# A fused attention, state-space and expert layer on one core: a chunk's preparation two slots forward, one expert layer per slot, and half of the key masks on ScalarE

## The chip, the cores and the metric

The kernel runs on one core of a Trainium2 chip. The metric is the device time of one execution in microseconds, as the median of several executions. Engines are named as in the profile: PE is TensorE, DVE is VectorE, ACT is ScalarE, POOL is GpSimd, SP is SyncE, which only issues DMAs here.

## The reference, cut to what matters

The input is four images of 64x64 tokens with 64 channels, all float32.

```python
h = window_attention(x)                    # 8x8 windows, 8 heads of 8 channels, 2D rotary, output projection
h = h + mamba(layernorm(h))                # RMS norm, in-projection to xc and z, causal conv over 4 taps, silu
#   delta = softplus(xc @ Wd + bd); dA = exp(delta * A); state h_t = dA_t*h_{t-1} + x_t*delta_t*B_t
#   y = (sum over 16 states of h_t*C_t + xc*D) * silu(z); out projection, residual
h = h + experts(layernorm(h))              # router of 6 experts, top 2; each expert has 3 layers with relu
```

## The kernel before, in words

The 16384 tokens are cut into 16 chunks of 1024 (CH). One call of `body(c, odd)` on each engine is one chunk's time of 32 slots (SLOTS), numbered n. Every engine has its own `body`, with its own order of helper calls inside a slot; the order of instructions on an engine is therefore written out by hand, and the engines meet through semaphores only. Six bodies run ahead of the hardware loop (c = -3 to 2), the loop does c = 3 to 12 two chunks at a time, and five more bodies close (c = 13 to 17).

A slot n of body c holds work of up to five chunks:

- **The scan of chunk c**, one unit (8 channels by 16 states, half a chunk of time) per slot. ACT writes the decay of unit n+2 to PSUM (`decay`, L767; it waits for the scan of unit n). DVE scans unit n (L1005) and multiplies B into a later unit (`feed`, L996). POOL multiplies with C (`weigh`, L1252). PE gathers four units at a time (`collect`, L449). SP loads `dl` for unit n+5 and `xd` for unit n+6, each broadcast to 128 partitions.
- **The attention of chunk c+3** (from slot 9; slots 0 to 8 finish chunk c+2, by `attention_at`), in its own slots s = n-9. PE turns the input (s=0), makes keys and queries (`keys_queries`, s=1 and 3, L466 and L470) and values (s=5, 6). DVE rotates them into `rot` (L1033, s=2 and 3) and POOL adds the two parts (L1265, s=4, which is slot 13). SP then copies the 16 head blocks of the keys into `k_heads` (`heads`, L341: 2 window halves by 8 heads, 6, 5 and 5 of them in slots 13, 14, 15) and the two halves of the queries into `q_diag` (`queries`, L350, slot 14). `k_heads` has, for every head, 64 key columns that are zero outside the head's 8 channels. The scores of window w (`scores`, L527, s = 9+2w, the first of them in slot 18) wait for all 18 of these DMAs. DVE takes the maximum (`maxima`, L1023, two slots on), ACT spreads it into `shift`, PE makes the transposed scores (`turned`, L537 and L538), ACT the exponentials (`probsT`, L775), PE the values (`values`, L551), ACT copies them out (`pv`).
- **The preparation of chunk c+1** (`prepare` on PE, ACT, DVE and POOL): transposes of the normed input (n0, n1 in slots 4, 5), the convolution (conv0, conv1 in slots 6, 7; L571 and L572 on PE, L844 on ACT), z (slots 8, 9), silu between two loads of activation tables (slot 9, L757 and L853), delta's projection (slots 11, 12; L863 and L864), exp and log of softplus (slot 13, L867), xdel's first step on DVE (slot 14, L1072) and eight steps on POOL (slots 14 to 21, L1301 to L1308). SP writes delta and xdel to DRAM (`keep`, slots 20 and 22). The second half of C is made in slot 2 of the chunk's own body (`second`: PE L594, ACT c_rep).
- **The normalisation of chunk c+2** (`normalize`), and **the experts of chunk c-1** (`experts`, `layers`, `route`): the output projection mo (PE L608, slot 4), the norm, the router (DVE `route`, slots 15 to 19: some twenty short operations, L1110 to L1166), then three pairs of experts with two layers each (h1_0, h2_0, ..., h2_2). A layer fills two PSUM banks, bank 7 (F) and bank 6 (G). LAYERS_PE says in which slot PE makes a layer and whether early or late in it; LAYERS_ACT says for each of the two banks when ACT empties it. Both halves of a table are served by the two calls of `layers` in the PE and ACT bodies.

Bank 6 also serves n0, n1, conv0, conv1, z0, d0, d1, c0 and c1, so each of these waits until ACT has emptied the one before; z1 is in bank 7, with the F uses.

```python
def attention_at(c, n):
    return (c + 3, n - 9) if n >= 9 else (c + 2, n + 23)
```

Of the kernel before, what the change touches and what calls it, by code (L numbers as in the profile page):

```python
# [21 lines left out]
NW = IMG // WIN  # L22
# [16 lines left out]
        ("keep", NCH + 1)]  # L39
ONCE = [("bv_rep", 128), ("wp_row", 64), ("normw", 1), ("conv_in", 128), ("conv_tap", 256), ("z_in", 128),  # L40
        ("d_skip", 1), ("a_log", NU), ("rb1", 1), ("rw2", E), ("headmask", 8)]
# [22 lines left out]
for _w in range(NW):  # L64
# [12 lines left out]
LAYERS_ACT = {(14, False): ("h1_0", 0), (14, True): ("h1_0", 1), (16, True): ("h2_0", 0), (17, False): ("h2_0", 1),  # L77
              (17, True): ("h1_1", 0), (18, False): ("h1_1", 1), (19, False): ("h2_1", 0), (19, True): ("h2_1", 1),
              (20, False): ("h1_2", 0), (20, True): ("h1_2", 1), (21, False): ("h2_2", 0), (21, True): ("h2_2", 1)}
# [38 lines left out]
def tower(nc, x, packed, select, out):  # L118
    with ExitStack() as ctx:
# [114 lines left out]
        heads_in = sig("heads_in", 18 * 16)  # L234
# [70 lines left out]
        def _(sp):  # L305
# [60 lines left out]
            def body(c, odd):  # L366
                for n in range(SLOTS):
# [15 lines left out]
                    if has(c + 1):  # L383
                        if n == 20:
                            keep(c + 1, 0)
                        if n == 22:
                            keep(c + 1, 1)
# [37 lines left out]
        def _(pe):  # L425
# [95 lines left out]
            def scores(k, w):  # L521
# [3 lines left out]
                if w == 0:  # L525
                    pe.wait_ge(heads_in.sem, heads_in.at(k, 288))
# [29 lines left out]
            def prepare(k, q, n):  # L556
                for s, i2 in ((4, 0), (5, 1)):
# [7 lines left out]
                for h in range(2):  # L565
                    at = BAND * h
                    if n == 6 + h:
# [6 lines left out]
                    if n == 8:  # L574
# [8 lines left out]
                    if n == 11 + h:  # L583
# [12 lines left out]
            def second(k, q, n):  # L596
                if n == 2:
# [68 lines left out]
            def layers(k, n, late, before):  # L666
                name = LAYERS_PE.get((n, late))
# [43 lines left out]
            def body(c, odd):  # L711
# [4 lines left out]
                for n in range(SLOTS):  # L716
# [22 lines left out]
                    if has(c - 1):  # L739
                        layers(c - 1, n, True, before_layers)  # L740
# [716 lines left out]
```

## Time and profile before

| | |
|---|---|
| median of 3 runs | 2001.69 us (1990.23 to 2002.55) |
| the profiled execution's own time | 2010.24 us |
| its span in the profile | 2008.4 us |
| instructions | 31457 |
| busy share of the span | PE 71%, DVE 66%, POOL 60%, ACT 52% |
| granted TensorE clock, mean | 0.779 of full speed |

The profile is of one execution. A row of a timeline gives start, duration, engine, line, operation, tiles, count, and in brackets how long the engine stood idle before it and what ended that. Each engine's rows stand in the order in which its body issues them, so a slot can be found by counting the scans (L1005) or POOL's L1252. The first scan of chunk 0 starts near 225 us; before it three bodies hold attention and preparation alone.

### The profile page before, as it was taken

The numbers are of one execution on the slowest core, as the hardware profiler recorded it, in microseconds if no ns is written. First come the engines' busy times: TensorE is split into PE (matmuls) and PEld (weight loads), VectorE is DVE, ScalarE is ACT, GpSimd is POOL, SyncE is SP. The second block draws the span as 40 slices with busy tenths as digits, with TensorE's granted clock in tenths as the row PEclk, the third lists the DMA queues.
The fourth block names the chain that finished last, engine by engine and source line by source line (L and its number), as shares of the span: only waits on it lengthen the run. The fifth ranks groups of instructions, "written<-read, shape, count | busy, mean of one in ns | idle before, by whom it ended". The sixth has DMA issues, their size and how long they took to land. (4 is left out here: it accounts for less than half of the span.)

```text
span 2008.4 us, 31457 instructions
## 1 busy us (share of the span) xinstructions
PE 1430.9 (71%) x8148; PEld 654.9 (33%) x8148; DVE 1327.5 (66%) x1835; ACT 1049.3 (52%) x1956; POOL 1207.1 (60%) x1665
## 2 busy tenths in 40 slices
PE   3655757796977777686868777686868778566566
PEld 1442424252433334242423334242433334121121
DVE  1111568777678776877677776878577776868851
ACT  1223556546565654656565654656465655554432
POOL 1003375756667674766677674766567675877651
PEclk9776968777788877787988877787887878675755
DMA  2000556554656564555646465555546565676720
GB/s 63 2 16 28 165 183 207 162 162 141 190 148 207 159 194 145 167 177 149 190 145 203 149 198 148 168 178 152 176 136 202 159 188 153 191 202 205 215 78 6
DMA packets 223979, 306.55 MB, mean 153 GB/s; under 512 B 88141, under 2 KB 88345, under 8 KB 223641
## 3 DMA queue, kind: packets, MB, share of 16 engines
q1 hardware_dynamic: 223768, 304.19, 50.5%
q8 instruction: 78, 1.28, 0.3%
q14 instruction: 133, 1.08, 0.2%
HBM read 274.75 MB, written 20.97 MB: 147 GB/s over the span
## 5 line engine op out<-in xcount | busy, mean ns | idle before, releaser
L1252 POOL TENSOR_TENSOR hc<-hs,c_rep 128x512 f32<-128x512 f32 x512 | 654.7, 1279 | 539.8 <-DVE hs L1005 539.8
L1005 DVE TENSOR_TENSOR_SCAN hs<-bank,state,xd 128x512 f32<-128x512 f32 x512 | 651.5, 1275 | 38.1 <-issue 15.6
L767 ACT ACTIVATE bank<-dl,a_neg 128x512 f32<-128x512 f32 x512 | 350.5, 687 | 186.2 <-DVE hs L1005 167.2
L996 DVE TENSOR_TENSOR xd<-xd,bank 128x512 f32<-128x512 f32 x512 | 336.9, 663 | 49.0 <-PE bank L439 43.2
L527 PE MATMUL bank<-k_heads,q_diag 128*128 128x512 f32 x256 | 182.8, 804 | 145.5 <-DMA k_heads<-rot 103.3
L1023 DVE TENSOR_REDUCE neg_max<-bank 128x8 f32<-128x512 f32 x128 | 88.2, 689 | 266.2 <-PE bank L527 255.0
L537 PE MATMUL bank<-q_diag,k_heads 128*128 128x128 f32 x1024 | 212.3, 333 | 20.7 <-ACT shift L760 20.7
L537 PEld LDWEIGHTS bank<-q_diag,k_heads 128*128 128x128 f32 x1024 | 182.8, 217 | 98.6 <-issue 63.7
L775 ACT ACTIVATE probsT<-bank 128x512 f32<-128x512 f32 x128 | 76.4, 597 | 240.5 <-PE bank L538 240.5
L449 PE MATMUL bank<-hc,wts 128*32 128x512 f32 x1024 | 169.3, 721 | 6.4 <-POOL hc L1252 6.2
L1324 POOL TENSOR_TENSOR ew<-ew,e 128x512 f32<-128x512 f32 x96 | 121.3, 1264 | 55.0 <-ACT e L760 55.0
L684 PE MATMUL bank<-fT,wts 64*128 64x512 f32 x192 | 81.7, 939 | 99.6 <-ACT ew L942 82.1
L538 PE MATMUL bank<-ident_b,shift 128*128 128x128 bf16 x512 | 121.2, 237 | 0.0
L527 PEld LDWEIGHTS bank<-k_heads,q_diag 128*128 128x128 f32 x256 | 47.2, 226 | 202.9 <-issue 95.4
L551 PE MATMUL bank<-v_diag,probsT 128*64 128x18 f32 x2048 | 85.6, 217 | 36.3 <-ACT probsT L775 32.0
L551 PEld LDWEIGHTS bank<-v_diag,probsT 128*64 128x64 f32 x2048 | 73.7, 142 | 99.9 <-issue 58.1
L760 ACT ACTIVATE shift<-neg_max 128x512 bf16<-128x512 f32 x128 | 79.5, 621 | 38.8 <-DVE neg_max L1023 38.8
L1033 DVE SCALAR_TENSOR_TENSOR rot<-bank,wts 128x512 f32<-128x512 f32 x64 | 45.1, 746 | 74.5 <-PE bank L470 74.2
L594 PE MATMUL bank<-xz,wts 128*128 128x512 f32 x128 | 85.7, 757 | 8.7 <-ACT xz L853 7.7
L571 PE MATMUL bank<-xnT,conv_w 128*128 128x512 f32 x64 | 54.4, 945 | 40.4 <-ACT xnT L760 27.1
L939 ACT ACTIVATE e<-bank,wts 128x512 f32<-128x512 f32 x96 | 62.7, 675 | 38.4 <-PE bank L684 38.1
L760 ACT ACTIVATE pv<-bank 128x72 f32<-128x72 f32 x128 | 29.4, 230 | 92.6 <-PE bank L551 90.9
(175 smaller groups left out, 2442.1 us busy)
## 6 DMA issues: line engine op xcount, KB each, us to landing
xd<-xdel_rows SPq DMA_DIRECT2D x512, 256.0 KB, 3.9
dl<-delta_rows SPq DMA_DIRECT2D x512, 256.0 KB, 3.6
delta_rows<-delta SPq DMA_DIRECT2D x16, 512.0 KB, 4.3
xdel_rows<-xdel SPq DMA_DIRECT2D x16, 512.0 KB, 4.4
xin<-in_x_dram SPq DMA_DIRECT2D x32, 128.0 KB, 2.5
k_heads<-rot SPq DMA_DIRECT2D x256, 16.0 KB
q_diag<-rot SPq DMA_DIRECT2D x32, 128.0 KB
out_dram<-res SPq DMA_DIRECT2D x256, 16.0 KB
```

What stands on the lines that cost most here:

```text
L449: last = pe.matmul(y_ps[32 * g:32 * g + 32, :], col("y_sel", 32 * i, 32 * i + 32), hc[:, n % 8, :], start=False, stop=True, skip_group_che ...
L527: pe.matmul(use.bank[:, :], q_diag[:, w, :], k_heads[:, w, :, :], start=True, stop=True)\
L537: pe.matmul(use.bank[:, at], k_heads[:, w, 2 * hp:2 * hp + 2, :], q_diag[:, w, :], start=True, stop=True)
L538: last = pe.matmul(use.bank[:, at], shift[:, w % 2, 2 * hp:2 * hp + 2, :], ident_b[:, :], start=False, stop=True, skip_group_check=True)
L551: last = pe.matmul(use.bank[64 * par:64 * par + 64, 18 * hp:18 * hp + 18], probsT[:, w % 2, 128 * hp + 64 * par:128 * hp + 64 * par + 64], ...
L760: return act.activation(out_, in_, ACT.Copy)
L767: act.activation(decay_ps[n % 2][:, :], dl[:, n % 4, :], ACT.Exp, scale=a_neg[:, g:g + 1])\
L996: dve.tensor_tensor(xd[:, n % 8, :], xd[:, n % 8, :], b_ps[:, :], ALU.mult).then_inc(injected.sem, 1)
L1005: dve.tensor_tensor_scan(hs[:, n % 4, :], decay_ps[n % 2][:, :], xd[:, n % 8, :], state[:, g:g + 1], ALU.mult, ALU.add).then_inc(scanned.s ...
L1023: dve.tensor_reduce(neg_max[:, w % 2, :], use.bank[:, :].rearrange("p (h j) -> p h j", h=HEADS), X_AXIS, ALU.max, negate=True).then_inc(us ...
L1252: pool.tensor_tensor(hc[:, n % 8, :], hs[:, n % 4, :], c_rep[:, BAND * h:BAND * h + BAND], ALU.mult)\
L1324: pool.tensor_tensor(ew[:, j, :], ew[:, j, :], wb[:, i % 2, :], ALU.mult).then_inc(weighed.sem, 1)
```

## The change

- `prepare` and `second` are two slots earlier on PE, ACT, DVE and POOL: n0, n1 in slots 2, 3; conv in 4, 5; z in 6 (PE) and 6, 7 (ACT); silu with its table loads in 7; delta in 9, 10; exp and log in 11; L1072 in 12; POOL's eight steps in 12 to 19; `keep` in 18 and 20. c1 is made by PE in slot 0 and emptied by ACT in slot 1. Not moved: POOL's residual add (slot 6) and c0 (slot 22).
- `layers` is called once per slot. PE makes one layer in each of slots 15 to 20, late in the slot; ACT empties both of its banks in the next slot. In bank 7 the router's logits (lg) come before h1_0.
- The keys' blocks of heads 4 to 7 are still copied by SP, 8 DMAs, four each in slots 13 and 14. Heads 0 to 3 are written by ACT in slots 14 and 15, two each, as a copy of all 128 partitions of `rot` with a per-partition scale of one or zero (`headmask`, which is now kept in SBUF). The scores of window 0 wait for 10 DMAs and 4 ACT operations; so does DVE before it overwrites `rot`.
- In ACT's body, `attend` and the new `heads` now come before `prepare`.

```diff
-        ("keep", NCH + 1)]
+        ("keep", NCH + 1), ("headmask", 8)]
...
-F_USES = [(n, 0) for n in ("mo", "fT", "r", "h1_0", "lg", "h2_0", "h1_1", "h2_1", "h1_2", "h2_2", "wT", "outT", "out")]
-LAYERS_PE = {(13, True): "h1_0", (16, False): "h2_0", (17, False): "h1_1", (18, True): "h2_1", (19, True): "h1_2",
-             (20, True): "h2_2"}
-LAYERS_ACT = {(14, False): ("h1_0", 0), (14, True): ("h1_0", 1), (16, True): ("h2_0", 0), (17, False): ("h2_0", 1),
...
+F_USES = [(n, 0) for n in ("mo", "fT", "r", "lg", "h1_0", "h2_0", "h1_1", "h2_1", "h1_2", "h2_2", "wT", "outT", "out")]
+LAYERS = ("h1_0", "h2_0", "h1_1", "h2_1", "h1_2", "h2_2")
+LAYERS_PE = {15 + _i: _n for _i, _n in enumerate(LAYERS)}
+LAYERS_ACT = {16 + _i: _n for _i, _n in enumerate(LAYERS)}
...
-        heads_in = sig("heads_in", 18 * 16)
+        heads_in = sig("heads_in", 10 * 16)
+        heads_act = sig("heads_act", HEADS // 2)
...
-                    half, h = i // HEADS, i % HEADS
+                    half, h = i % 2, HEADS // 2 + i // 2
...
-                        if 13 <= n < 16:
-                            heads(c + 3, *((0, 6), (6, 11), (11, 16))[n - 13])
+                        if 13 <= n < 15:
+                            heads(c + 3, 4 * (n - 13), 4 * (n - 12))
...
-                        if n == 20:
+                        if n == 18:
                             keep(c + 1, 0)
-                        if n == 22:
+                        if n == 20:
                             keep(c + 1, 1)
...
-                    pe.wait_ge(heads_in.sem, heads_in.at(k, 288))
+                    pe.wait_ge(heads_in.sem, heads_in.at(k, 160))
+                    pe.wait_ge(heads_act.sem, heads_act.at(k, HEADS // 2))
...
-                for s, i2 in ((4, 0), (5, 1)):
+                for s, i2 in ((2, 0), (3, 1)):
...
-                    if n == 6 + h:
+                    if n == 4 + h:
...
             def second(k, q, n):
-                if n == 2:
+                if n == 0:
...
                     if has(c - 1):
-                        layers(c - 1, n, False, before_layers)
                         experts(c - 1, n)
...
-                        layers(c - 1, n, True, before_layers)
+                        layers(c - 1, n, before_layers)
...
+            def heads(k, s):
+                if s in (5, 6):
+                    for h in (2 * s - 10, 2 * s - 9):
+                        if h == 0:
+                            act.wait_ge(roped.sem, roped.at(k, 1))
+                        act.activation(k_heads[:, :, h, :], rot[:, 1, :].rearrange("p (w j) -> p w j", w=NW), ACT.Copy,
+                                       scale=col("headmask", h, h + 1)).then_inc(heads_act.sem, 1)
...
                     if has(c - 1):
-                        layers(c - 1, n, False)
+                        layers(c - 1, n)
                         experts(c - 1, n)
                     if has(c - 2):
                         experts(c - 2, SLOTS + n)
+                    if has(k):
+                        attend(k, s)
+                        heads(k, s)
                     if has(c + 1):
                         prepare(c + 1, 1 - odd, n)
-                    if has(k):
-                        attend(k, s)
                     if has(c + 2):
                         normalize(c + 2, n)
-                    if has(c - 1):
-                        layers(c - 1, n, True)
...
-                if n == 14:
+                if n == 12:
...
-                if 14 <= n < 22:
-                    step, h = (n - 14) // 2, n % 2
+                if 12 <= n < 20:
+                    step, h = (n - 12) // 2, n % 2
```

## Rows read from the trace of the kernel before

**Rows 1.** The page, part 1: busy time and share of the span
```profile
PE 1430.9 (71%) x8148; PEld 654.9 (33%) x8148; DVE 1327.5 (66%) x1835; ACT 1049.3 (52%) x1956; POOL 1207.1 (60%) x1665
```
**Rows 2.** The waits of the whole span: us in total, times, longest
```profile
DVE neg_max L1023 <- PE bank L527: 255.0, 76, 17.8
...
PE bank L527 <- DMA k_heads<-rot: 103.3, 16, 14.7
```
**Rows 3.** PE timeline: the first scores of bodies -3, -1, 0 and 8
```profile
43.39 2.05 PE L527 MATMUL bank<-k_heads,q_diag 128*128 128x512 f32 x2 [13.68 <-DMA k_heads<-rot]
...
197.30 2.05 PE L527 MATMUL bank<-k_heads,q_diag 128*128 128x512 f32 x2 [14.66 <-DMA k_heads<-rot]
...
285.28 2.05 PE L527 MATMUL bank<-k_heads,q_diag 128*128 128x512 f32 x2 [10.13 <-DMA k_heads<-rot]
...
1167.29 2.07 PE L527 MATMUL bank<-k_heads,q_diag 128*128 128x512 f32 x2 [4.06 <-DMA k_heads<-rot]
```
**Rows 4.** SP timeline: DMA issues of body -3, and the first in body 8
```profile
28.48 8.19 SPq L341 DMA_DIRECT2D k_heads<-rot  x11
36.72 1.37 SPq L350 DMA_DIRECT2D q_diag<-rot  x2
38.13 3.69 SPq L341 DMA_DIRECT2D k_heads<-rot  x5
...
1149.01 4.49 SPq L341 DMA_DIRECT2D k_heads<-rot  x6
```
**Rows 5.** DVE timeline, body 0, slots 18 to 20
```profile
283.51 0.69 DVE L996 TENSOR_TENSOR xd<-xd,bank 128x512 f32<-128x512 f32 x1 [4.84 <-DMA xd<-xdel_rows]
...
287.36 0.69 DVE L1023 TENSOR_REDUCE neg_max<-bank 128x8 f32<-128x512 f32 x1 [2.57 <-PE bank L527]
```
**Rows 6.** Windows, slots 14 to 20 of body 8: PE, PEld, DVE, ACT, POOL busy, then clock, DMA, GB/s
```profile
1148.00:1175.00 27.00, 15.01 (x85) 5.24 (x85) 24.38 (x44) 14.04 (x30) 22.24 (x32) 0.72 0.47 131
```
**Rows 7.** DVE timeline, body 8, slots 8, 9, 11, 14, 15 and 20
```profile
1126.74 0.69 DVE L1086 TENSOR_REDUCE st_f<-fsq 128x8 f32<-128x512 f32 x1 [2.73 <-ACT fsq L897]
...
1132.47 0.69 DVE L1051 TENSOR_TENSOR hid<-bank,h_bias 128x512 f32<-128x512 f32 x1 [3.28 <-PE bank L517]
...
1140.49 1.41 DVE L1033 SCALAR_TENSOR_TENSOR rot<-bank,wts 128x512 f32<-128x512 f32 x2 [3.19 <-PE bank L470]
...
1149.16 1.61 DVE L1072 TENSOR_SCALAR xdel<-ex_d 128x1024 f32<-128x1024 f32 x1 [1.10 <-ACT ex_d L867]
...
1151.28 1.27 DVE L1005 TENSOR_TENSOR_SCAN hs<-bank,state,xd 128x512 f32<-128x512 f32 x1
...
1172.91 0.69 DVE L1023 TENSOR_REDUCE neg_max<-bank 128x8 f32<-128x512 f32 x1
```
**Rows 8.** ACT timeline, body 8: n0, conv1, first table load, silu, xT
```profile
1117.32 1.61 ACT L760 ACTIVATE xnT<-bank 64x256 f32<-64x256 f32 x4 [2.71 <-PE bank L431]
...
1129.31 0.69 ACT L844 ACTIVATE xz<-bank,wts 128x512 f32<-128x512 f32 x1 [2.60 <-PE bank L572]
...
1133.39 1.28 ACT L757 ACT_TABLE_LOAD   x1
1134.68 1.91 ACT L853 ACTIVATE xz<-xz 128x2048 f32<-128x2048 f32 x1
...
1137.91 0.60 ACT L760 ACTIVATE xT<-bank 128x512 f32<-128x512 f32 x1
```
**Rows 9.** PE timeline, body 8: mo in slot 4
```profile
1113.68 2.20 PE L608 MATMUL bank<-wts,y_gated 128*128 128x64 f32 x16
```
**Rows 10.** One line each: durations min/median/max in ns, first and last start
```profile
L1137 DVE SCALAR_TENSOR_TENSOR rt<-rt x16: 207/1184/1186, 376.2 to 1968.1; 128x48 f32<-128x48 f32 x16
...
L572 PE MATMUL bank<-xnT,conv_w x64: 590/1061/1062, 158.7 to 1790.5; 128*128 128x512 f32 x64
...
L1301 POOL TENSOR_TENSOR xdel<-xdel,ex_d x32: 1260/1267/1277, 184.7 to 1810.5; 128x512 f32<-128x512 f32 x32
...
L885 ACT ACTIVATE bank<-xz,d_col x32: 672/674/688, 236.3 to 1912.5; 128x512 f32<-128x512 f32 x32
```

More of the change, by code:

```diff
@@ L573, in prepare @@
                           .then_inc(use.filled, 1)
-                    if n == 8:
+                    if n == 6:
                         use = Bk[f"z{h}"]
@@ L664, in weights, with layers @@
                       .then_inc(use.filled, 1)
-            def layers(k, n, late, before):
-                name = LAYERS_PE.get((n, late))
+            def layers(k, n, before):
+                name = LAYERS_PE.get(n)
                 if name:
@@ L823, in prepare @@
             def prepare(k, q, n):
-                for s, i2 in ((4, 0), (5, 1)):
+                for s, i2 in ((2, 0), (3, 1)):
                     if n == s:
@@ L838, in prepare @@
                 for h in range(2):
-                    if n == 6 + h:
+                    if n == 4 + h:
                         use = Bk[f"conv{h}"]
@@ L845, in prepare @@
                            .then_inc(use.drained, 1)
-                    if n == 8 + h:
+                    if n == 6 + h:
                         use = Bk[f"z{h}"]
@@ L855, in prepare @@
                 for h in range(2):
-                    if n == 11 + h:
+                    if n == 9 + h:
                         use = Bk[f"d{h}"]
@@ L873, in second @@
             def second(k, q, n):
-                if n == 2:
+                if n == 1:
                     rep(k, "c1", 1)
@@ L929, in experts, with layers @@
                     copy(outT[:, :], use.bank[:, :]).then_inc(use.drained, 1)
-            def layers(k, n, late):
-                if (n, late) in LAYERS_ACT:
-                    name, s = LAYERS_ACT[n, late]
+            def layers(k, n):
+                name = LAYERS_ACT.get(n)
+                if name:
                     what, e = name.split("_")
                     e = int(e)
-                    use = (F, G)[s][name]
-                    act.wait_ge(use.filled, use.full(k))
-                    if what == "h1":
-                        act.activation(e1[:, s, :], use.bank[:, :], ACT.Relu, bias=col("eb1", e, e + 1)).then_inc(use.drained, 1)
-                    else:
-                        bias = eb2_x[:, e:e + 1] if s else col("eb2", e, e + 1)
-                        act.activation(ew[:, EP * s + e, :], use.bank[:, :], ACT.Relu, bias=bias).then_inc(use.drained, 1)
+                    for s, use in enumerate((F[name], G[name])):
+                        act.wait_ge(use.filled, use.full(k))
+                        if what == "h1":
+                            act.activation(e1[:, s, :], use.bank[:, :], ACT.Relu, bias=col("eb1", e, e + 1))\
+                               .then_inc(use.drained, 1)
+                        else:
+                            bias = eb2_x[:, e:e + 1] if s else col("eb2", e, e + 1)
+                            act.activation(ew[:, EP * s + e, :], use.bank[:, :], ACT.Relu, bias=bias).then_inc(use.drained, 1)
+            def heads(k, s):
[5 more added lines that the diff above has]
+                                       scale=col("headmask", h, h + 1)).then_inc(heads_act.sem, 1)
             def shift_out(k, s):
@@ L1031, in attend @@
                         if name == "k" and past(k - 1):
-                            dve.wait_ge(heads_in.sem, heads_in.at(k - 1, 288))
+                            dve.wait_ge(heads_in.sem, heads_in.at(k - 1, 160))
+                            dve.wait_ge(heads_act.sem, heads_act.at(k - 1, HEADS // 2))
                         dve.scalar_tensor_tensor(
@@ L1061, in prepare @@
             def prepare(k, n):
-                if n == 3:
+                if n == 1:
                     if past(k - 1):
```

14 lines of the change are left out of this document (6 added, 8 removed).

## The prediction

> **What bounds the kernel now.** I read the page first, then the waits, then timelines of single bodies. No engine is full: PE is busy 71% of the span, DVE 66%, POOL 60%, ACT 52% [rows 1]. So the time lies in how four engines with fixed orders wait for each other, and a wait counts only where nothing later in the same body would have been late anyway. The waits of the whole span put two beside this change [rows 2]: DVE waits 255.0 us for scores (L1023 for L527), and PE waits 103.3 us in 16 pieces, one per body with attention, for the DMAs into k_heads.
>
> The 16 pieces are not alike. In body -3 nothing but attention runs: PE stands idle 13.68 us before the first scores at 43.39, in body -1 14.66 us [rows 3]. In body 8 the wait is 4.06 us and the scores start at 1167.29 [rows 3], but DVE reaches the maximum that reads them only at 1172.91, with no idle before it [rows 7]. From 1148 to 1175 DVE is busy 24.38 of 27.00 us [rows 6]. That stretch (slots 14 to 20: scans plus the router) belongs to DVE, and this DMA wait is hidden there.
>
> DVE's idle in body 8 lies before it: 2.73 us in slot 8, 3.28 in slot 9, 3.19 in slot 11, 1.10 in slot 14 [rows 7], 10.3 in all. Its cause is the preparation: a chain that goes between PE and ACT through one PSUM bank, and ends in ACT's block of table load, silu, table load, from 1133.39 until xT is copied at 1137.91 [rows 8]. Keys and queries wait for xT, DVE's rotation waits for them.
>
> **Part 1, key blocks, where the first scores are exposed.** SP needs 8.19 us for 11 head DMAs [rows 4], 0.74 each. Eight fewer save 5.96 us of issuing, and all 16 are needed before the first scores: in body -3 the last is issued by 38.13 + 3.69 = 41.82 and the scores start at 43.39, 1.6 us later. With eight DMAs and the queries (1.37), issued from 28.48, I get 28.48 + 5.9 + 1.4 + 1.6 = 37.4 against 43.39: 6.0 us gained. ACT's four masks need the same rotated keys; the nearest row is L885, a 128x512 copy with a scale per partition, 0.674 us [rows 10]. Four are 2.7 us beside 7.3 us of issuing, on an engine that idles there. Bounds of one mask, since it reads and writes SBUF with rows of 64: 0.67 as that row, and 1.27 as POOL's L1301 from SBUF to SBUF [rows 10]; four are 2.7 to 5.1, under 7.3 either way. I take 0.67. So bodies -3 and -2 give 6.0 each.
>
> Body -1 also prepares chunk 0. Its chain starts two slots, thus one window's scores and values, earlier; xT no longer stands behind silu's second table load. I take 3 us for that (bounds 0, and the 4.5 us of ACT's block [rows 8]) and 6.0 for the key blocks: 9.0.
>
> In body 0 scans run but no router. SP is blocked by the head DMAs for so long that xd comes late (4.84 us of DVE idle), then DVE waits 2.57 for the scores of 285.28 [rows 3, 5]. Six us fewer of issuing end both but for about 1.4: 6.0. Sum of the four: 6 + 6 + 9 + 6 = 27 us.
>
> In bodies 1 to 12 I cost the DMA part at nothing. The router on DVE hides it; without that cover it would be worth up to 4.06 us [rows 3]. The masks there are 2.7 us in ACT's slots 14 and 15, in the stretch where ACT is busy 14.04 of 27 us [rows 6]; the next decay behind them has two scans of DVE as slack. Cost 0, bound 2.7. SP's issue of dl and xd is freed of 6 us, which can only help.
>
> **Part 2, preparation two slots forward (bodies 0 to 14).** I follow body 8. c1 moves one PE matmul pair into slot 0 and out of slot 2, and ACT's copy out of the path pv to shift in slot 2: about as much lost in one as gained in the other, 0 (bounds -1 and +1). PE is at mo at 1113.68 for 2.20 us [rows 9], as before. Now n0 and n1 are already done, beside the last windows (ACT 1.61 us each [rows 8], while PE makes scores and values). So conv0 follows mo at 1115.9. Each conv is four matmuls; L572 has a median of 1.061 and a minimum of 0.590 us [rows 10], the two levels of TensorE's clock, 1.2 and 2.4 GHz. At the slow one, 3.8 us with overlap: conv0 done 1119.7, emptied by ACT (0.69) 1120.4; conv1 behind a gather 1125.0, emptied 1125.7, against 1130.0 before [rows 8]. z's matmuls, a decay, fsq, the copy of att and two z copies follow: the table load at 1129.3 instead of 1133.39. The block of 4.5 us ends at 1133.8.
>
> What is late next: the decay of unit 10 is now behind that block, and scans 7 and 8 wait for decays behind the convs. DVE gets new idle of about 1.2, 3.6 and 2.9 us in slots 7, 8 and 10 in place of most of 2.73 + 3.28 + 3.19. After the block ACT makes two decays, three small ones and xT: done 1136.2 against 1138.5. PE makes keys and queries until 1138.2, DVE rotates at 1138.7 against 1140.49 [rows 7]: 1.8 us won. L1072 (1.61) moves from slot 14 to 12, in front of the second rotation, and waits some 0.5 for exp; the scan of slot 15 starts at 1149.5 against 1151.28. So 1.8 us stay. Bounds: 0, and the 4.1 us by which ACT's block moves. Fifteen bodies: 27 us.
>
> **Part 3, POOL's eight steps in slots 12 to 19.** They are 1.267 us each [rows 10]. Two leave slots 20 and 21 and two come into 12 and 13, next to the rotary adds. POOL, busy 22.24 of 27.00 [rows 6], then has hardly a gap while DVE runs the router. That matters by the rows: L1137, a 48-element operation with two SBUF inputs, has a minimum of 207 ns and a median of 1184 ns [rows 10]; the minimum is in the closing body, where POOL is idle, and the difference of 0.98 us is a wait for POOL's operation. I take one more such wait per body, 1.0 us in 14 bodies (1 to 14): 14 us lost. Bounds: 0, and the eight router operations of that kind which now start freely, 7.8 us.
>
> The Trainium skill has this as a rule (SBUF — State Buffer, "Who interferes with whom"): a VectorE instruction with two SBUF inputs contends with a GpSimd instruction that reads SBUF, and the order of issue decides who blocks. The row agrees. By the rule alone each of the eight could wait; by this row only as often as POOL has no gap.
>
> **Part 4, layers one per slot.** The same matmuls and copies. In slot 20 the chain is unchanged: scan 20, decay, shift, both copies of h1_2, then h2_2, then the transposed scores. lg no longer waits for h1_0. In the closing body lg's bank must be empty before h1_0: +0.5. Cost 0; cover is the router on DVE, and without it a layer would cost at most one copy of 0.69 late per slot.
>
> **Sum.** 27 + 27 - 14 = 40 us. The profiled execution would go from 2010.24 (span 2008.4) to 1970. It lies 8.6 above the median of 2001.69; taken off that, 1962 us.
>
> **The rivals.**
>
> *A, TensorE at its fast level in the preparation.* The slow conv rows come after idle of PE between banks. With scores and mo packed against the preparation, PE idles less, and the convs could run at 2.4 GHz: 4 x (1.061 - 0.590) = 1.9 us per conv, 3.8 per body [rows 10]. Against it: the bank still goes back and forth. Taking 2.5 of the 3.8 on the path: 1962 - 15 x 2.5 = 1925.
>
> *B, the wait only moves.* DVE's new waits for decays eat the 1.8 us, while the 14 us of part 3 offset a remainder: the steady bodies give nothing, the start its 27. 2002 - 27 = 1975.
>
> *C, slower: POOL saturated under the router.* If several of the eight free operations wait 0.98 us each, the loss per body is 3.9 for four, and four is the point from which it decides: 14 x 3.9 = 55 against 54 gained. With five, 2002 - 54 + 69 = 2017; with all eight 2058. For it: POOL already has only 4.8 us free in 27 [rows 6]. Against it: POOL still has to wait for DVE's scans.
>
> *D, no change: the key blocks don't pay.* If ACT's masks come late (queue behind v's copies, or writes much slower than 1.27 us) the first scores start no sooner: 1962 + 27 = 1989.
>
> **How the numbers follow.** Forecast 0.45 (1945 to 1978), A 0.17, B 0.20, C 0.08, D 0.10. A measurement of this kernel can tell about 1%, here 20 us, from no change. Below 1981.7: all of A, nearly all of the forecast, most of B: 0.75. Above 2021.7 or near it, C: 0.08. Within 1%: the rest, 0.17. The range leaves out the lower part of A (all 3.8 us won in each body, 1905) and C: 1922 to 1992.
>
> **What would show it.** The first scores in body -3 start near 37.4, in body -1 some 9 us or more earlier than 197.30 less the 12 us already won, in body 0 the 4.84 us wait for xd is gone. In body 8, counted from its first scan: table load 4 us earlier, rotation 2 us earlier without idle before it, new idle of DVE in slots 8 and 10 ended by ACT, the median of more router lines at 0.6 to 1.2 us. PE's wait for k_heads falls from 103.3 to under 35 us in total. I am wrong if a steady pair of bodies takes as long as before, if conv rows have their median at 0.59 (A), or if DVE's busy time rises by more than 50 us (C).

## Result, and the profile after

The changed kernel takes 1930.09 us in the median of 4 runs (1921.91 to 1949.11), the one before 2002.12 (1990.23 to 2011.94, 4 runs). The ratio is 0.966 with a 95% interval of 0.957 to 0.974. Forecast were 1962 us, a gain of 40; it is 72. The side and the range hold, the size doesn't. In some executions of a kernel the whole run takes over 1.5% longer than in its fastest; ratios leave these out, medians here take all in.

The page of the changed kernel, part 1 (engine, busy us, share of the span, instructions):

```profile
span 1920.1 us, 31423 instructions
...
PE 1396.5 (73%) x8148; PEld 648.9 (34%) x8148; DVE 1341.6 (70%) x1835; ACT 1086.1 (57%) x2020; POOL 1209.0 (63%) x1665
```

Against [rows 1] ACT is busy 36.8 us longer (64 masks more), DVE 14.1 (the router, as shown below), and PE 34.4 less: the same 8148 matmuls, more of them at the fast level. The span is 88.3 us shorter. By the first scan of each chunk, the gain is made up so: 17.0 us lie ahead of chunk 0 (first scan at 207.9 against 224.9), 25.7 in bodies 0 to 2, 35.4 in bodies 3 to 12, 7.3 in bodies 13 and 14, 2.7 behind.

PE's timeline, first scores of bodies -3, -1 and 0:

```profile
38.38 2.05 PE L528 MATMUL bank<-k_heads,q_diag 128*128 128x512 f32 x2 [8.47 <-DMA q_diag<-rot]
...
178.05 2.05 PE L528 MATMUL bank<-k_heads,q_diag 128*128 128x512 f32 x2 [8.69 <-DMA q_diag<-rot]
...
258.90 2.05 PE L528 MATMUL bank<-k_heads,q_diag 128*128 128x512 f32 x2 [3.55 <-issue]
```

In [rows 3] the waits were 13.68, 14.66 and 10.13 us. What ends the first two now is the queries' DMA, the last to be issued (for the third the profile names nothing). All waits of PE for a DMA at the scores sum to 25.5 us in three pieces, where there were 103.3 us in 16 [rows 2]. In body -3 SP gives the eight key blocks in 6.01 us (0.75 each), then the queries until 36.10, and the scores start 2.3 us later. In body 0 DVE's wait for xd is shorter, not gone:

```profile
261.30 0.69 DVE L1005 TENSOR_TENSOR xd<-xd,bank 128x512 f32<-128x512 f32 x1 [3.07 <-DMA xd<-xdel_rows]
```

ACT in body 8 (first scan at 1049.33), then DVE's rotation and the one long idle time before it:

```profile
1057.33 1.61 ACT L760 ACTIVATE xnT<-bank 64x256 f32<-64x256 f32 x4
...
1067.54 0.69 ACT L844 ACTIVATE xz<-bank,wts 128x512 f32<-128x512 f32 x1 [1.56 <-PE bank L573]
...
1072.16 1.28 ACT L757 ACT_TABLE_LOAD   x1
1073.45 1.91 ACT L853 ACTIVATE xz<-xz 128x2048 f32<-128x2048 f32 x1
...
1078.40 0.57 ACT L760 ACTIVATE xT<-bank 128x512 f32<-128x512 f32 x1
```

```profile
1071.20 0.69 DVE L1096 TENSOR_REDUCE st_f<-fsq 128x8 f32<-128x512 f32 x1 [0.44 <-ACT fsq L897]
...
1077.45 1.28 DVE L1014 TENSOR_TENSOR_SCAN hs<-bank,state,xd 128x512 f32<-128x512 f32 x1 [3.20 <-issue]
...
1081.60 1.40 DVE L1043 SCALAR_TENSOR_TENSOR rot<-bank,wts 128x512 f32<-128x512 f32 x2
```

Counted from the body's first scan (1101.74 before), the table load stands at 22.8 us instead of 31.7 [rows 8], the rotation at 32.3 instead of 38.8 [rows 7]. The scan of slot 10 waits 3.20 us, where 2.9 were foreseen. The profile names no releaser; I read it as the wait for the decay that ACT makes behind the tables, from 1076.68 on.

PE in body 8, slots 16 to 20:

```profile
1099.20 0.28 PE L694 MATMUL bank<-e,wts 128*32 128x8 f32 x2 [5.12 <-ACT e L939]
...
1103.19 2.08 PE L685 MATMUL bank<-fT,wts 64*128 64x512 f32 x4
1105.20 1.15 PE L528 MATMUL bank<-k_heads,q_diag 128*128 128x512 f32 x2
...
1111.90 1.91 PE L685 MATMUL bank<-fT,wts 64*128 64x512 f32 x4 [4.03 <-ACT ew L943]
1113.74 2.00 PE L528 MATMUL bank<-k_heads,q_diag 128*128 128x512 f32 x2
1117.60 0.23 PE L694 MATMUL bank<-e,wts 128*32 128x8 f32 x2 [1.86 <-ACT e L939]
```

In this body the scores wait for no DMA any more, but PE stands idle all the same, now in front of the layers, whose inputs ACT empties. And the same matmul L528 takes 1.15 us in one row and 2.00 in the next: the two levels of the clock.

The table below is mine, worked out from DVE's scans in the one profile of each kernel: the mean time in us of each stretch of slots in bodies 3 to 11.

| slots | 0-4 | 5-11 | 12-19 | 20-23 | 24-31 | body |
|---|---|---|---|---|---|---|
| before | 13.2 | 29.3 | 31.8 | 11.6 | 26.3 | 112.2 |
| after | 13.8 | 22.1 | 31.9 | 13.2 | 28.2 | 109.2 |

Slots 5 to 11, the preparation, give 7.2 us; slots 20 to 31, the scores, take 3.5 of them back. Neither was forecast at this size. The experiments ask for both. Inside slots 12 to 19, which look unchanged, slots 12 to 14 give 1.6 us and slots 15 to 19, the router, take 1.7 more (22.3 before, 24.0 now).

### The profile page after: what moved, and what is told of

It is laid out like the page before. It is cut to its first block and busy times, and to the rows that moved or that the text cites. A ratio compares the mean times of both kernels' runs of the same rounds, so it can differ in the third digit from the quotient of the medians.

```text
span 1920.1 us, 31423 instructions
## 1 busy us (share of the span) xinstructions
PE 1396.5 (73%) x8148; PEld 648.9 (34%) x8148; DVE 1341.6 (70%) x1835; ACT 1086.1 (57%) x2020; POOL 1209.0 (63%) x1665
## 3 DMA queue, kind: packets, MB, share of 16 engines
q14 instruction: 140, 1.15, 0.2%
## 5 line engine op out<-in xcount | busy, mean ns | idle before, releaser
L538 PE MATMUL bank<-q_diag,k_heads 128*128 128x128 f32 x1024 | 226.4, 348 | 6.0 <-ACT shift L760 4.5
L538 PEld LDWEIGHTS bank<-q_diag,k_heads 128*128 128x128 f32 x1024 | 193.8, 229 | 82.8 <-issue 65.5
L528 PE MATMUL bank<-k_heads,q_diag 128*128 128x512 f32 x256 | 175.1, 772 | 56.3 <-DMA q_diag<-rot 25.5
L449 PE MATMUL bank<-hc,wts 128*32 128x512 f32 x1024 | 182.8, 777 | 4.0 <-POOL hc L1262 2.6
L539 PE MATMUL bank<-ident_b,shift 128*128 128x128 bf16 x512 | 125.3, 245 | 0.0
L694 PE MATMUL bank<-e,wts 128*32 128x8 f32 x96 | 11.6, 194 | 126.5 <-ACT e L939 126.5
L528 PEld LDWEIGHTS bank<-k_heads,q_diag 128*128 128x128 f32 x256 | 48.5, 225 | 118.2 <-issue 55.0
L698 PE MATMUL bank<-e,wts 64*64 64x512 f32 x384 | 76.2, 875 | 0.0
L1278 POOL TENSOR_TENSOR att<-pv,rec 128x512 f32<-128x512 f32 x16 | 17.2, 1075 | 92.3 <-DVE rec L1052 92.3
```

Of the source, the lines that this page charges most:

```text
L449: last = pe.matmul(y_ps[32 * g:32 * g + 32, :], col("y_sel", 32 * i, 32 * i + 32), hc[:, n % 8, :], start=False, stop=True, skip_group_che ...
L528: pe.matmul(use.bank[:, :], q_diag[:, w, :], k_heads[:, w, :, :], start=True, stop=True)\
L538: pe.matmul(use.bank[:, at], k_heads[:, w, 2 * hp:2 * hp + 2, :], q_diag[:, w, :], start=True, stop=True)
L539: last = pe.matmul(use.bank[:, at], shift[:, w % 2, 2 * hp:2 * hp + 2, :], ident_b[:, :], start=False, stop=True, skip_group_check=True)
```

## The experiments

In the expectations T1 mostly stands for "the level of TensorE's clock decides", T2 for "the order of the work decides"; fill_both words its T2 and T3 itself. The kernel before was measured again beside the runs: 2008.79 us for the first four, 2000.08 for POOL's steps back, fill_before, fill_start and fill_both, 1998.30 for the others. The ratios go by these; the changed kernel was not measured again.

### One part alone

**Preparation alone** (`prepare`, `second`, `keep`, POOL's steps, and ACT's `attend` first; key blocks and layers as before):

```diff
-                for s, i2 in ((4, 0), (5, 1)):
+                for s, i2 in ((2, 0), (3, 1)):
...
-                    if n == 6 + h:
+                    if n == 4 + h:
```

> The kernel before with the preparation, the second half of C, keep and POOL's eight steps two slots forward, and ACT's attention ahead of its preparation; key blocks and layers as before. Three theories. T1, the clock: in the profile of the changed kernel the stretch from slot 5 to the end of slot 11 takes 22.1 us in every steady body against 29.3 before, and TensorE's granted clock in it is 0.89 to 1.0 against 0.63 to 0.88; most of that gain comes with the clock, because the preparation now follows on scores, and the part that does it is this one. Then this kernel has slots 5 to 11 at 22 to 24 us, the L572 matmuls at 0.59 us in the median, and is 60 us or more below the kernel before (about 1940). T2, structure as the prediction had it: 1.8 us a body, 27 us less 14 for the router's collisions, about 1990, L572 still near 1.06. T3, the clock is kept by the key blocks or the layers, not by this part: slots 5 to 11 stay above 26 us and the time is 1985 or more. The start-up until the first scan of chunk 0 shortens by 3 us or less in all three.

1966.54 us, ratio 0.979 (0.969 to 0.989): 42 us won, between the 60 of T1 and the 13 or so of T2. The profile is of its slowest execution, 1996.66, whose first scan comes 21 us later than in the profile before; the slots of the bodies are read from it all the same. Slots 5 to 11 take 22.1 us, as in the changed kernel, and the convolution's median is at the fast level (first row; the second is the kernel with the key blocks alone):

```profile
L572 PE MATMUL bank<-xnT,conv_w x64: 589/591/1061, 179.4 to 1769.6; 128*128 128x512 f32 x64
```

```profile
L574 PE MATMUL bank<-xnT,conv_w x64: 590/1057/1061, 159.5 to 1826.7; 128*128 128x512 f32 x64
```

So this part alone makes the preparation's gain. The router's slots 15 to 19 take 24.1 us here too. Slots 20 to 31 take 42.2 us against 37.9 before: it brings the loss too.

Its profile holds a by-product. Bodies -3 have the same instructions here and before, and PE's timelines are alike until 50 us; then, the scores of window 2, first here, then in the kernel before:

```profile
52.84 2.08 PE L527 MATMUL bank<-k_heads,q_diag 128*128 128x512 f32 x2 [0.32 <-ACT pv L760]
```

```profile
52.48 1.13 PE L527 MATMUL bank<-k_heads,q_diag 128*128 128x512 f32 x2 [0.32 <-ACT pv L760]
```

With the same instructions and the same waits the clock had risen in one execution and not in the other. A window then takes 4.06 or 6.59 us, the last of the eight maxima starts at 73.96 or 87.90, and the stretch before the first scan of chunk 0 is anywhere between 201 and 246 us in the profiles of this study. Two kernels that have the same instructions up to there, the changed one and the one with POOL's steps back (below), show it too: in body -2 their eight maxima are spread over 28.5 and 42.6 us, and the first scan comes at 207.9 and 221.5. A single profile can't tell a start-up gain under some 15 us.

**Key blocks alone** (8 DMAs and four masks on ACT):

> The kernel before with the key blocks alone: 8 DMAs in place of 16, four masks on ACT. By the steps of the prediction: first scores of body -3 near 38 (the changed kernel had 38.38), first scan of chunk 0 some 14 to 18 us earlier, body 0 another 6, the steady bodies unchanged within 1 us: 24 to 27 us in all, 1975. By theory T1 with a supplement (scores that no longer wait keep TensorE busy, or on the contrary open a gap behind them) the steady bodies change too: 1 to 2 us each either way, 1960 or 1995. If the start-up gain needs the moved preparation, the first scan of chunk 0 comes only 10 to 12 us earlier.

2035.33 us, ratio 1.014 (1.004 to 1.023): slower than before by an interval that leaves out 1, and not the 1975 expected. The first scores did start at 37.98. The bodies lost: bodies 3 to 12 take 1178 us against 1124, slots 20 to 31 43.3 against 37.9. PE in body 10, slots 18 to 21, here and then before:

```profile
1404.95 1.12 PE L529 MATMUL bank<-k_heads,q_diag 128*128 128x512 f32 x2
...
1414.05 2.08 PE L686 MATMUL bank<-fT,wts 64*128 64x512 f32 x4 [4.92 <-ACT ew L944]
1416.06 2.07 PE L529 MATMUL bank<-k_heads,q_diag 128*128 128x512 f32 x2
1419.74 0.27 PE L695 MATMUL bank<-e,wts 128*32 128x8 f32 x2 [1.61 <-ACT e L941]
...
1421.86 0.79 PE L539 MATMUL bank<-q_diag,k_heads 128*128 128x128 f32 x2
```

```profile
1395.96 2.08 PE L527 MATMUL bank<-k_heads,q_diag 128*128 128x512 f32 x2 [4.03 <-DMA k_heads<-rot]
...
1401.51 2.08 PE L684 MATMUL bank<-fT,wts 64*128 64x512 f32 x4 [1.35 <-ACT ew L942]
...
1407.75 0.49 PE L537 MATMUL bank<-q_diag,k_heads 128*128 128x128 f32 x2
```

Without the DMA wait the first scores come 3.6 us sooner behind the body's first scan, and PE idles later, 4.92 us in one piece before the layer of slot 19. The transposed scores, at the fast level before (0.49 for the first two), now come at the slow one (0.79), and DVE waits 6.09 us for the scores in slot 23 instead of 3.18. The removed wait was hidden; that much the prediction had. What it lacked is where the idle went.

**Layers alone:**

> The kernel before with the layers alone: one pair of experts' layers in each of slots 15 to 20, both banks emptied in the next slot. By the prediction nothing, 2002 within 10. A rival from the changed kernel's trace: there PE stands idle 5.12, 4.03 and 1.86 us in slots 16, 19 and 20, and slots 20 to 31 take 3.6 us more a body than before; if the layers behind ACT are what opens these gaps, this kernel loses 1 to 3.6 us in each of 14 bodies, 2015 to 2050, with the loss in slots 20 to 31. If emptying both banks together helps as it seems meant to, 5 to 15 us less than before.

2006.26 us, ratio 1.000 (0.995 to 1.005), slots 20 to 31 at 38.5 (37.9 before). Nothing, as forecast.

**All but the layers:**

> The changed kernel with the layers as before (preparation two slots forward and key blocks on ACT kept). If the layers are worth nothing: 1930, as the changed kernel. If the layers' new order makes the gaps of PE in slots 16 to 20 and so the 3.6 us a body that slots 20 to 31 gave back: about 1930 less 20 to 50, that is 1880 to 1910, with slots 20 to 31 at 37.9 us as before and not 41.4. If the layers' order is what makes room for the preparation (ACT's copies in slots 14 to 21), 1940 to 1960.

1945.36 us, ratio 0.962 (0.951 to 0.972), within the interval of the changed kernel. Slots 20 to 31 stay at 41.0, so the new order of the layers isn't what gives back there. The 1880 to 1910 expected for that case are missed. Preparation (-42) and key blocks (+27) don't add: together -63. With the preparation moved forward the key blocks do no harm: slots 20 to 31 already take 42.2 us with the preparation alone. Which of PE's idle times makes this so is not shown.

**POOL's steps back in slots 14 to 21** (the changed kernel otherwise):

```diff
-                if 12 <= n < 20:
-                    step, h = (n - 12) // 2, n % 2
+                if 14 <= n < 22:
+                    step, h = (n - 14) // 2, n % 2
```

> The changed kernel with POOL's eight steps back in slots 14 to 21 and keep back in 20 and 22; nothing else. Part 3 of the prediction says that these steps under the router cost 1.0 us a body; slots 15 to 19 did take 24.0 us in the changed kernel against 22.3 before. If the prediction holds, the router goes back to about 22.3 us, and this kernel is 14 to 24 us below the changed one (1906 to 1916), as long as xdel, which is now written two slots later, is still in DRAM in time for the next chunk. Rival, the level of TensorE's clock decides: the gain in slots 15 to 19 appears, and slots 20 to 31 take it back or double it depending on the clock, so the total is anywhere within 20 us of 1930. Rival, slower: SP's keep waits for POOL's last step, and the slot after it loads xd late, 1940 to 1960.

1911.46 us, ratio 0.954 (0.947 to 0.962); the intervals of this and of the changed kernel overlap. The total is as expected, its reason is not: slots 15 to 19 take 23.9 us here and 24.0 in the changed kernel, where 22.3 were expected. One router line is at 1184, 209 and 1191 ns in the median in the kernel before, the changed one and this one; the last two:

```profile
L1147 DVE SCALAR_TENSOR_TENSOR rt<-rt x16: 207/209/1202, 345.1 to 1876.3; 128x48 f32<-128x48 f32 x16
```

```profile
L1147 DVE SCALAR_TENSOR_TENSOR rt<-rt x16: 207/1191/1199, 357.0 to 1872.4; 128x48 f32<-128x48 f32 x16
```

A median hides how often each of two values comes, so I summed the nine such lines body by body. In bodies 3 to 11 they take 6.8 us before, 8.4 in the changed kernel, 8.0 here and 7.4 with the preparation alone, each line 0.2 or about 1.2 us. So the change does make the router longer, and to put the eight steps back takes away some 0.3 us of the 1.5. What brings the rest, the phase in which DVE meets POOL for instance, was not tested. The 1.9 us a body that this kernel wins are 0.5 in slots 12 to 14 and 1.5 in slots 24 to 31.

### The clock by itself

The fillers keep the order and only give PE something to do while it waits: matmuls into a free bank whose result nobody reads.

```python
def warm(bank, times):
    for _ in range(times):
        pe.matmul(bank[:, :], ident, wts[:, 0:BAND], start=True, stop=True)
```

**Kernel before, filler ahead of the convolutions and of the keys (fill_before):**

> The kernel before, nothing moved: one unread matmul call ahead of each convolution (PE idles 1.69 and 0.85 us there) and two ahead of the keys (4.56 us idle). It tells how much of the preparation's 7.2 us a body is the clock alone. T1: the convolutions go to the fast level (L572's median 0.59 us instead of 1.06), slots 5 to 11 from 29.3 to 25 or 26 us, 30 to 55 us in all (1950 to 1975). If the 7.2 us are the new order of the work, slots 5 to 11 stay at 29 within 1 us and the time at 2000 or some us above.

2008.16 us, ratio 1.003 (0.999 to 1.007). All convolutions are fast (median 590 ns) and the first table load of body 8 comes at 28.8 us instead of 31.7, but slots 5 to 11 take 29.8 us, the 29 expected if the order decides. Yet the run doesn't speak for the order. The two calls ahead of the keys stood behind the wait for the queries' bank, which is the one that ACT copies xT from; so they started at 33.9, when the keys could have, and held these until 37.1. The gain and this delay cancel. So the run was made again with the convolutions' filler only (fill_conv):

```diff
                         use = Bk[f"conv{h}"]
+                        if past(k - 2):
+                            pe.wait_ge(F["mo"].drained, F["mo"].empty(k - 2))
+                        if past(k - 1):
+                            pe.wait_ge(Bk["z1"].drained, Bk["z1"].empty(k - 1))
+                        warm(Bk["z1"].bank, 1)
                         fill(use, k)
```

> The kernel before with the unread matmuls ahead of the two convolutions alone; the two ahead of the keys, which began only when ACT had copied xT and so pushed the keys back by 3.2 us, are gone. In the earlier run the convolutions at the fast level brought the first table load in body 8 from 31.7 to 28.8 us behind the first scan. So, if the clock's share of the preparation is those 2.9 us: slots 5 to 11 at 26 to 27 us in place of 29.3, and 25 to 40 us in all, 1962 to 1977. If the later slots give it back (the scores stage starts sooner but at the slow level), 1985 to 2000.

1957.89 us, ratio 0.979 (0.971 to 0.986). Body 8 of this kernel, PE ahead of and in conv0, and the first table load, 28.0 us behind the first scan at 1057.42:

```profile
1074.59 1.02 PE L459 MATMUL bank<-wts 128*128 128x512 f32 x2
1076.45 1.12 PE L580 MATMUL bank<-xnT,conv_w 128*128 128x512 f32 x2 [0.84 <-ACT xnT L769]
1077.42 1.02 PE L581 MATMUL bank<-xnT,conv_w 128*128 128x512 f32 x2
...
1090.66 0.25 PE L470 MATMUL bank<-xT,wts 128*32 128x8 f32 x2 [4.57 <-ACT xT L769]
1090.84 1.99 PE L474 MATMUL bank<-xT,wts 64*64 64x512 f32 x8
```

```profile
1085.40 1.28 ACT L766 ACT_TABLE_LOAD   x1
```

Slots 5 to 11 take 26.1 us. Of the preparation's 7.2 us, 3.2 are to be had by the clock alone, with nothing moved. The other 4.0 are not the order of the work alone, for the first call of keys and queries is still slow here (1.99 us, last row above), and in the changed kernel it is fast:

```profile
1079.24 1.09 PE L470 MATMUL bank<-xT,wts 64*64 64x512 f32 x8
```

So 3.2 is a lower bound of the clock's share and 4.0 an upper bound of the order's; no run makes both fast with nothing moved. Some 9 of the 40 us that this run wins lie elsewhere, in slot 1 of bodies 5, 7, 9 and 11, where the next two runs look.

**Changed kernel, filler ahead of the first scores of bodies -3 to 0 (fill_start):**

```diff
+                if w == 0 and isinstance(k, int) and k < 4:
+                    warm(use.bank, (4, 4, 4, 2)[k])
                 if w == 0:
```

> The changed kernel with matmuls whose results nobody reads, written into the bank of the first scores while PE waits for the heads: 4 calls of 128x512 f32 in bodies -3, -2 and -1 and 2 in body 0, about 2.1 us each at the slow level, beside waits of 8.5 and 3.6 us. In the profiles so far, with the same instructions in body -3, a window took 4.06 us in one execution and 6.59 in another, the scores' matmul 1.13 against 2.07: the level of the clock. Theory T1, the clock is kept by what PE did before: the windows of bodies -3 and -2 take 4.06 us from the first or second on, their eight maxima end within 32 us in every profile, and the median falls by 8 to 20 us against the changed kernel, with a smaller spread of its runs. Rival, the level is set by something that does not depend on this: no change within 5 us, and windows of 6.59 us still appear. The filler itself costs at most 0.5 us a body.

1903.65 us (1900.17 to 1907.81), ratio 0.952 (0.945 to 0.959). The expected size, but the reason holds by half: in body -3 a window takes 4.06 us once the third is through, in body -2 all but the first take 6.59. Most of the gain lay elsewhere: in the first bodies of the loop's second to fifth pass (5, 7, 9, 11), slot 1 took 7.2 to 7.9 us and now 3.2 to 3.9. PE in body 7 of the changed kernel, at the loop's head:

```profile
939.19 0.65 PE L552 MATMUL bank<-v_diag,probsT 128*64 128x18 f32 x16 [0.96 <-DVE neg_max L1032]
942.74 2.07 PE L595 MATMUL bank<-xz,wts 128*128 128x512 f32 x2 [2.90 <-issue]
```

PE waits 2.90 us for nothing that the profile shows, and is at the slow level behind it. The control (shift_code) has as many instructions as that filler, in the setup, where they fill no gap of a body:

```diff
+            for _ in range(14):
+                pe.matmul(psum[5][0:32, 0:8], col("y_sel", 0, 32), wts[:, 0:8], start=True, stop=True)
```

> The changed kernel with 14 calls of 32x8 matmuls, read by nobody, in PE's setup, where it waits for the first input: as many instructions as the filler at the start had, but no work in the gaps. It separates two readings of that run (26 us below the changed kernel). Reading 1: in every first body of the loop (5, 7, 9, 11) PE stood idle 2.6 to 3.7 us right behind the loop's head, with nothing that it waited for, and slot 1 took 7.2 to 7.9 us instead of 3.2; with the filler at the start the gap is gone (3.2 to 3.9), so where the loop's instructions lie decides. Then this kernel has slot 1 at 3.2 to 3.9 in those bodies too and is 15 to 20 us below the changed one, about 1912. Reading 2: the filled gaps keep the clock up and this removes the gap: then this kernel is the changed one, 1930, with slot 1 at 7 to 8 in the odd bodies.

1914.79 us, ratio 0.957 (0.951 to 0.963). Its body 7:

```profile
946.03 0.65 PE L552 MATMUL bank<-v_diag,probsT 128*64 128x18 f32 x16 [0.96 <-issue]
946.60 1.13 PE L595 MATMUL bank<-xz,wts 128*128 128x512 f32 x2
```

The gap is gone, slot 1 takes 3.2 to 3.6 us, and the four bodies win 16.9 us in this slot. So 28 instructions ahead of the loop, which do no work in it, decide over that gap (reading 1); that it is a matter of where the loop's instructions lie is the natural reading of this. Body 3, the first pass, has no such gap in any kernel. The kernel before has it too (4.6 to 6.3 against 2.4), 8.5 us less over the four bodies than the changed kernel. Variants with more or fewer instructions can move this gap too (21.3 to 30.7 us for the four slots in the kernels without a filler), so some us of the differences in this document, the 72 included, are of this kind. The interval of this run's ratio overlaps that of the changed kernel; what is shown is the gap.

**Changed kernel, the same filler and in slots 16, 19 and 20 (fill_both):**

```diff
+                        if has(k) and n in {16: 2, 19: 1, 20: 1}:
+                            pe.wait_ge(A["v1"].drained, A["v1"].empty(k))
+                            warm(A["T0"].bank, {16: 2, 19: 1, 20: 1}[n])
                         layers(c - 1, n, before_layers)
```

> As the run before, and in every body with layers the same kind of unread matmuls in the gaps of PE in slots 16, 19 and 20 (5.12, 4.03 and 1.86 us idle in body 8 of the changed kernel): two, one and one calls. Theory T1: the drops of the clock in these slots come from the idle; without them slots 20 to 23 go from 13.2 to about 11.6 us and slots 24 to 31 from 28.2 towards 23 to 26, that is 3 to 6 us in each of 13 bodies, 1870 to 1890 in all with the filler at the start. Rival T2, the drop that costs (slots 27 to 31) comes from what PE does there itself, with no idle before it: slots 24 to 31 stay at 28 and the time equals that of the run before within 10 us. Rival T3: the filler delays layers and scores by its own length at the slow level (up to 2 us where the gap is 1.86), 5 to 20 us slower.

1871.47 us, ratio 0.932 (0.922 to 0.943), inside what T1 expected. Slots 20 to 23 take 12.0 us and 24 to 31 26.0: together 37.9, what they took in the kernel before. Of the wide matmuls in slots 20 to 31 (over 0.5 us each) 26% took over 0.85 us in the changed kernel, 33% with the filler at the start, and 9% here. shift_code, whose loop is moved too, keeps 41.8. So PE's idle in slots 16 to 20 is what gave back the 3.5 us a body. T2 and T3 of that run are out.

**Key blocks alone, two calls in slot 19 (h_gap):**

> The kernel with the key blocks alone (2035, 27 above the one before) and two unread matmul calls in PE's gap of 4.92 us in slot 19. In that kernel the gap of 4.06 us before the first scores was gone and the gap before the layer of slot 19 was 4.92 instead of 1.35; the clock was slow from 63.9 to 81.0 us behind the first scan of body 8, where the one before had it back at 75.0. If that later idle is what made slots 20 to 31 take 43.3 us instead of 37.9: here they take 37 to 39, and the time is 1965 to 1985. If the loss comes from the order of scores and layers itself, the time stays at 2025 or more.

2039.57 us in the fastest execution, which is the profiled one, and 2073.95 to 2091.35 in the other three (median 2077.90). Even the fastest lies 41 us above the kernel before, and slots 20 to 31 take 44.3 us, where 37 to 39 were expected. A miss: by the words of the expectation it speaks for the order of scores and layers as the cause. It doesn't settle that either, for in body 10 two idle times of 2.4 and 2.7 us are left around the layers, and the transposed scores are slow again. That idle costs in the kernel with the key blocks alone is thus argued from its rows, not shown.

**Changed kernel, POOL's steps back, all fillers, one more call in slot 18:**

> The changed kernel with both that paid: POOL's eight steps back in slots 14 to 21, the filler at the start, and unread matmuls in PE's gaps of slots 16 (two), 18, 19 and 20 (one each). If the two gains add, 1871 less 10 to 19: 1852 to 1861. If they share the same slots (the router's gain shows only as more idle before the scores), 1871. If a call in slot 18 is one too many at the slow level, 1875 to 1890.

1847.80 us (1840.20 to 1853.95), ratio 0.925 (0.919 to 0.931), faster than both kernels; its interval overlaps that of fill_both. Slots 20 to 31 take 37.5 us, the mean granted clock is 0.874. Page of this kernel, part 1:

```profile
span 1844.4 us, 31719 instructions
...
PE 1374.7 (75%) x8296; PEld 638.2 (35%) x8296; DVE 1335.7 (72%) x1835; ACT 1084.7 (59%) x2020; POOL 1207.3 (65%) x1665
```

PE has 148 matmuls more than the changed kernel and is busy 21.8 us less.

## Why the prediction was right and wrong

**Part 1, start-up.** First scores at 38.38 for 37.4: the step took 1.6 us from the last issue to the scores, as behind the last key block; behind the queries, which are last now, it is 2.3. The masks took 0.67 each, as costed. By the first scan of chunk 0, 17.0 us for the 21 of bodies -3 to -1, where the changed kernel had three slow windows in body -3 (2.5 us each) that the one before did not; so the 21 are in reach, and the runs can't tell more. Body 0: 7.0 us for the forecast 7.8, but by other terms. The waits for xd and for the scores were to fall from 7.41 us to 1.4; the latter is gone, the former is 3.07. Slots 12 to 19 give 4.7 us, the preparation's 5 to 11 give 3.2 for 1.8, and slots 20 to 23 lose 1.0. The sum came near by luck.

**Part 1, bodies 1 to 12, "I cost the DMA part at nothing".** The wait was hidden, as said, and the step still failed: alone, this part costs 1.4%. A wait that is hidden on DVE's side is an idle time of PE, and the rows of body 10 suggest that to move it changes PE's clock later (argued, see h_gap). In the changed kernel it has no share of its own that the runs show: slots 20 to 31 take 41.4 us, and 42.2 without the key blocks.

**Part 2, 1.8 us a body.** The step failed by its size: 7.2 us. Two terms were mis-sized. The convolutions were costed at the slow level, 3.8 us each. They ran fast, as rival A had it, for which 0.17 was given, and which the prediction named as a sign that it is wrong (conv rows with their median at 0.59); fill_conv puts this at 3.2 us a body (A took 2.5). And the new idle of DVE in slots 7, 8 and 10 was put at 1.2 + 3.6 + 2.9 = 7.7 us; it is 0.62 + 0.44 + 3.20 = 4.3. The order gives at most 4.0 us, near the upper bound of 4.1, and some of that is the keys' matmuls at the fast level.

**Part 3, one more wait of 0.98 us a body.** The effect came and is somewhat larger: the router's nine lines take 1.5 us more in bodies 3 to 11, slots 15 to 19 take 1.7 more, and DVE is busy 14.1 us longer in all. Its reason did not: with the two steps put back the nine lines are still 1.2 us longer than before, and with the preparation alone 0.5. The rows bear out that a two-input operation waits for POOL's (0.21 us in the closing bodies, where POOL is idle, 1.18 in the others), which is the rule of the Trainium skill (SBUF — State Buffer, "Who interferes with whom"); they don't bear out that moving two steps adds one such wait. What the loss of 1.7 us doesn't show in the total is that slots 12 to 14 give 1.6 back, part of it the 1.10 us for which DVE waited before L1072. Rival C (four and more such waits) is out.

**Part 4.** 0 forecast, 1.000 measured alone.

**What was left out.** Slots 20 to 31 had no term at all and cost 3.5 us a body, by estimate 49 us in 14 bodies. So the forecast of 40 lies within reach of the 72 only by errors of opposite sign, which is luck: a preparation worth 5.4 us a body more, a scores stage worth 3.5 less, and 0.6 lost in slots 0 to 4, most of it in the gap behind the loop's head. Then, bodies 1 and 2: 18.8 us for 1.6. In body 1, 5.8 of them lie in slots 24 to 31, which take 23.0 us when PE is fast throughout and 28.8 when it isn't; slots 24 to 31 of one kernel with the same instructions vary between 23.1 and 31.6 us from body to body, so I count such single bodies to the spread of the runs. The interval of the ratio is 1916 to 1951 us; the forecast's 1962 lies above it, and rivals B (1975) and D (1989) further, while A's 1925 is inside. For the preparation A was the better account; it too had no term for slots 20 to 31.

## What to carry to other kernels

Cost a move by what it does to PE's idle times too, those nobody waits for: an idle time that shifts, or grows into one long one, can double the duration of the matmuls behind it (2.00 us for 1.15 in slots 18 and 20 here). Before a part of a chain is made shorter, look which of its durations come in two values, and price both. Where PE must wait anyway and a bank is free, unread matmuls in the gap are a cheap test and can be the gain: in slots 16 to 20 they gave 32 us here (1903.65 to 1871.47), behind the wrong wait (fill_before) they cost what they won, and in the kernel with the key blocks alone they won nothing. A median of durations that come in two values misleads: sum them.

## What the runs showed that I had not expected

- The same instructions with the same waits ran at either level of the clock from one execution to another (1.13 and 2.08 us for one call in body -3), and stayed there for eight windows. The Trainium skill (TensorE: Matmul & The Clock Gate, Part 1: The HAM clock gate) calls the start of the fast level run-variable, and by this the trace agrees; it also puts the penalty of the ramp below 1% of a typical span. Eight windows at the slow level cost 13.9 us in one body here, 0.7% of the span, which agrees; but with the many drops of a kernel like this one the level is worth more, 1.7% for the fillers of slots 16 to 20 (1903.65 to 1871.47).
- Before its first record the granted clock is listed as 1.00, whatever the level: in the profile of the preparation alone from 52 to 90 us, while all of the windows' matmuls have the slow duration. Behind it, record and durations agree: in the kernel before the matmuls are slow again from 77.5 us on, and the listed clock is 0.84 in the us from 77 and 0.50 from 78. I read levels from durations.

```profile
52.00:60.00 8.00, 6.67 (x41) 4.79 (x40) 0.69 (x1) 2.09 (x5) 0.00 (x0) 1.00 0.01 2
```

- PE stood idle 2.6 to 4.2 us behind the head of a loop from its second pass on, and 28 small matmul instructions ahead of the loop took that away (16.9 us in four passes).
